# Dispatch of the last four bins: three quarters of the slots, instead of half, summed in the mixture and ahead of the third expert group

## The reference, cut to what matters

```python
x = x + gcn(layernorm(x))            # two GCN layers over 100000 edges, 6250 nodes, 768 features
xn = l2norm(layernorm(x))            # 6250 x 768
logits = xn @ phin                   # 6250 x 1024 (32 experts x 32 slots)
d_w = softmax(logits over slots of an expert)    # dispatch weights
c_w = softmax(logits over all 1024 slots)        # combine weights
slots = xn.T @ d_w                   # 768 x 1024, sum over all 6250 nodes   <- what is changed
h  = gelu(slots @ w1[e] + b1[e])     # per expert, hidden 384
eo = h @ w2[e] + b2[e]               # per expert, back to 768
x = x + c_w @ eo
```

## Time and profile before

| | us |
|---|---|
| median of 3 runs | 3303.42 (3299.69 to 3303.58) |
| the profiled execution, its own time | 3298.73 |
| its span | 3297.0 |
| PE busy | 3078.9 (93%) |
| DVE / ACT / POOL busy | 1898.3 / 1155.6 / 1869.7 |

### The profile page before, as it was taken

The page is one execution under the profiler, slowest core; times in us unless marked ns, Lnnn a source line. Parts: engine busy times, 40 slices in busy tenths (PEclk is TensorE's granted clock), DMA queues, the critical chain, the costliest instruction groups (busy, mean ns, idle before and its releaser), DMA issues. The chain is left out here.

```text
span 3297.0 us, 62639 instructions
## 1 busy us (share of the span) xinstructions
PE 3078.9 (93%) x21857; PEld 2070.2 (63%) x21857; DVE 1898.3 (58%) x3437; ACT 1155.6 (35%) x1578; POOL 1869.7 (57%) x1804
## 2 busy tenths in 40 slices
PE   3769999999999999789999999999999998689998
PEld 1347777878787878556666666666666653345665
DVE  7854545554444444277777777777777773102332
ACT  4842323233323232245444444444444441111000
POOL 3377777777777777377666666666666631100000
PEclk8989999999999999899999999999999999899999
DMA  8789999999999999599889998998999879998995
GB/s 310 271 320 372 335 340 332 340 337 331 339 335 340 339 341 331 184 336 348 309 308 311 308 310 309 309 310 307 309 309 311 309 250 338 315 327 230 268 229 141
DMA packets 344868, 1013.79 MB, mean 307 GB/s; under 512 B 147903, under 2 KB 157578, under 8 KB 335592
## 3 DMA queue, kind: packets, MB, share of 16 engines
q0 software_dynamic: 137376, 664.09, 57.5%
q1 hardware_dynamic: 195152, 312.01, 29.2%
q10 hardware_dynamic: 12040, 33.69, 3.2%
HBM read 873.96 MB, written 129.21 MB: 304 GB/s over the span
## 5 line engine op out<-in xcount | busy, mean ns | idle before, releaser
L1610 POOL DMA_INDIRECT xs<-table,idx x833 | 877.2, 1053 | 473.4 <-PE m_part L1787 277.1
L1065 POOL DMA_INDIRECT xs<-table,idx x833 | 899.1, 1079 | 306.8 <-issue 192.8
L1787 PE MATMUL m_part<-xs 128*128 128x512 f16 (+1 forms) x3332 | 585.6, 329 | 27.1 <-DMA xs<-table,idx 22.0
L1382 PE MATMUL a_part<-xs 128*128 128x512 f16 (+1 forms) x3332 | 591.3, 328 | 15.3 <-DMA xs<-table,idx 11.0
L1787 PEld LDWEIGHTS m_part<-xs 128*128 128x128 f16 x3332 | 417.8, 142 | 164.9 <-issue 43.3
L1382 PEld LDWEIGHTS a_part<-xs 128*128 128x128 f16 x3332 | 409.6, 142 | 135.2 <-issue 26.7
L1816 PE MATMUL m_ps_l<-xs,m_xT 128*128 128x512 f16 x1764 | 388.7, 379 | 0.4 <-issue 0.2
L1803 PE MATMUL m_ps_s<-dw_mem,xn_mem 128*128 128x512 f16 x1296 | 312.4, 381 | 3.1 <-DVE xs L1677 3.0
L1816 PEld LDWEIGHTS m_ps_l<-xs,m_xT 128*128 128x128 f16 x1764 | 172.0, 98 | 207.9 <-issue 1.5
L1332 PE MATMUL a_ps_o<-Ws,xs 128*128 128x512 f16 x1764 | 294.8, 326 | 1.3 <-ACT xs L1115 1.2
L1115 ACT ACTIVATE xs<-xs 128x128 f16<-128x128 f32 x294 | 88.6, 310 | 464.7 <-DVE xs L1266 460.4
(11 more groups left out here) (418 smaller groups left out, 3909.4 us busy)
## 6 DMA issues: line engine op xcount, KB each, us to landing
xs<-in_L_ffn_w_dram SPq DMA_DIRECT2D x64, 1152.0 KB, 10.3
xs<-table SPq DMA_DIRECT2D x98, 384.0 KB, 6.2
xs<-table,idx POOLq DMA_INDIRECT x1666, 5.8
cw_dram<-xs SPq DMA_DIRECT2D x49, 512.0 KB
table<-arena SPq DMA_DIRECT2D x49, 384.0 KB, 3.1
table<-xs SPq DMA_DIRECT2D x49, 384.0 KB, 4.7
xs<-x_pad SPq DMA_DIRECT2D x49, 384.0 KB, 6.1
x_dram<-xs SPq DMA_DIRECT2D x49, 384.0 KB, 5.5
```

The source lines that it names most:

```text
L1065: pool.indirect_dma_start(out=ring[:, t, :], out_offset=None, in_=table, in_offset=bass.IndirectOffsetOnAxis(ap=idx[:, k:k + 1], axis=0)). ...
L1382: mm = nc.tensor.matmul(part[:, bass.ds(to + a, z - a)], pick[:, i % 2, :, t], ring[:, n % RING, half * D + a:half * D + z], start=False, ...
L1610: pool.indirect_dma_start(out=ring[:, t, :], out_offset=None, in_=table, in_offset=bass.IndirectOffsetOnAxis(ap=idx[:, n:n + 1], axis=0)). ...
L1787: mm = nc.tensor.matmul(part[:, bass.ds(off + at, e - f)], pick[:, i % 2, :, t], ring[:, n % RING, half * D + f:half * D + e], start=False ...
```

## The change

The boundary between what `second_layer` sums for the last four bins and what the mixture sums moves from slot 512 to slot 256 (`LATE_AT`). In `second_layer` the 12 units of the last four bins get 256 columns instead of 512. In the mixture each late unit has 24 matmuls (512 and 256 columns in turn) instead of 12 of 512, and its add is 768 wide instead of 512. All six late units now stand behind `down_product(0)`, and `up_product(2)`, whose slots begin at 256, waits for all of them.

```diff
+LATE_AT = K // 4
...
+        def width(g):
+            return 512 if g < whole else LATE_AT
...
-                        v.tensor_tensor(slots[:, c, a:a + 512], slots[:, c, a:a + 512], ps_s[:, tile % 2, :], ALU.add).then_inc(added, 1)
+                        v.tensor_tensor(slots[:, c, a:a + width(g)], slots[:, c, a:a + width(g)], ps_s[:, tile % 2, 0:width(g)], ALU.add).then_inc(added, 1)
...
-                                mm = nc.tensor.matmul(ps_s[:, tile % 2, :], spread(xn[q % XN][:, xh, :], DC)[:, c, :], dw[:, q % DW, dh, a:a + 512],
+                                mm = nc.tensor.matmul(ps_s[:, tile % 2, 0:width(g)], spread(xn[q % XN][:, xh, :], DC)[:, c, :], dw[:, q % DW, dh, a:a + width(g)],
...
-        late_units = {0: (0, 1, 2), 1: (3, 4), 2: (5,)}
+        late_units = {0: range(DC)}
...
-                    v.tensor_tensor(slots[:, c, K // 2:K], slots[:, c, K // 2:K], ps_o[:, c % 2, 0:K // 2], ALU.add).then_inc(late_added, 1)
+                    v.tensor_tensor(slots[:, c, LATE_AT:K], slots[:, c, LATE_AT:K], ps_o[:, c % 2, 0:K - LATE_AT], ALU.add).then_inc(late_added, 1)
...
-                    if g == HG:
+                    if g == LATE_AT // P:
                         pe.wait_ge(late_added, DC)
...
-                            mm = nc.tensor.matmul(ps_o[:, c % 2, 0:K // 2], spread(xn[b % XN][:, xh, :], DC)[:, c, :], dw[:, b % DW, dh, K // 2:K],
-                                                  start=(b == LATE_BINS[0] and xh == 0 and dh == 0), stop=(b == LATE_BINS[-1] and xh == 1))
+                            for a, e in ((LATE_AT, LATE_AT + 512), (LATE_AT + 512, K)):
+                                mm = nc.tensor.matmul(ps_o[:, c % 2, a - LATE_AT:e - LATE_AT], spread(xn[b % XN][:, xh, :], DC)[:, c, :], dw[:, b % DW, dh, a:e],
+                                                      start=(b == LATE_BINS[0] and xh == 0 and dh == 0), stop=(b == LATE_BINS[-1] and xh == 1))
```

## The result

| | before | after |
|---|---|---|
| median of 20 runs, us | 3301.79 | 3306.69 |
| lowest, highest | 3293.87, 3308.03 | 3302.21, 3312.78 |
| profiled execution's time, span | 3298.73, 3297.0 | 3305.12, 3303.3 |

The ratio is 1.0016, 95% interval 1.001 to 1.0023: 4.9 us slower on the medians. The forecast was 1.6 us faster (3301.8), with a range up to 3306.5. Here "before" is the median of 20 runs; the forecast was added to the median of three, 3303.42.

A forecast was written before the change was run, and what follows sets the result against it. The prediction took the weight stream to bound the first four expert groups, and TensorE-VectorE handoffs the end of second_layer. -4.2 us there and +2.6 for an empty queue gave -1.6: 3303.42 to 3301.8 us, range 3298.0 to 3306.5.

The forecast's parts named there:

- Narrower units at the end: End of second_layer: shorter matmuls and adds make the last add end 4.2 us earlier.
- the bounds of 3.1 and 4.6: Gain at the block's end: 3.1 us if SyncE does not move, 4.6 if its moved last issue sets the end.
- First products: Start of the mixture: first up product keeps 5.77 us; nothing taken for earlier-issued biases, up to 1 us held against.
- rival B: Second_layer's gain smaller or lost in the first products (SyncE, clock, biases): 3304 to 3305.6 us; chance 0.23 together with D.
- Late units: Behind down product 0: six units of 3.90 us, 23.4 us in all; up product 2 waits about 1.2 us for VectorE.
- rival C: Added narrow matmuls in the late units cost up to 0.216 us each: 7.7 us more, 3309.5 us; chance 0.10.
- The load behind it: Down weights of group 2, requested after down product 1: queue runs dry at 2790.3, issue at 2791.2, 2.6 us lost.
- The sum: Whole kernel: -4.2 us from second_layer's end, +2.6 from the empty queue, together -1.6 us.
- the 0.2% to which the prediction gave 0.92: Whole kernel: chance 0.92 that the time stays within 0.2%, 6.6 us, of no change.

The follow-up runs named there:

- tail_only: Changed kernel with the mixture of before, so only second_layer's last four bins are summed 256 wide; ratio to before 0.9993 (0.9984 to 1.0002).
- order5: Changed kernel with turn 1 and down product 1 moved ahead of the sixth late unit and up product 2; ratio to before 1.0002 (0.9993 to 1.0011).
- fill: order5 with one late unit moved between up products 0 and 1; ratio to before 0.9993 (0.9984 to 1.0002).
- before_bias: Kernel before with the first expert group's hidden bias loaded at the end of second_layer; ratio to before 1.0004 (0.9995 to 1.0012).
- before_early: before_bias plus the third of second_layer's last four weight loads issued right behind the last write of cst; ratio to before 0.9997 (0.9988 to 1.0006).
- late_only: Changed kernel with second_layer of before (512 wide), so only the mixture's half of the change; ratio to before 1.0017 (1.0009 to 1.0026).
- after_early: Changed kernel with the first hidden bias and the third of second_layer's last four weight loads issued earlier; ratio to before 1.0001 (0.9992 to 1.001).

## Why the prediction was wrong, step by step

**Narrower units at the end.** Right: the adds end 4.0 us earlier (4.2 forecast; 3.5 to 3.6 in tail_only, order5 and fill). The block ends 3.5 us earlier, within the bounds of 3.1 and 4.6. In this trace that is because the landing of `cst` took 0.9 us longer and SyncE became the last; in the other three VectorE was the last and the gain was the same.

**First products: the step that failed.** "I take nothing for it and hold up to 1 us against it." Up product 1 waited 4.0 us instead of 0.67, and ran 1.7 us longer at the low clock. Down product 0 was forecast to end at 33.3 and ended at 39.0. The miss of 5.7 us is 0.7 (block end) + 3.3 (wait) + 1.7 (clock). I had followed SyncE's two last loads to their issue, as a thing that could end the block, but not to their landing, and had not asked who waits for it. up_product(1) does. In before they landed at 24.5, 3.7 us ahead of their user at 28.2 (some 2 us with up product 0 at the high clock). The gain of 3.5 us went nearly whole into this slack: the path to their issue leads through the softmax, the write of `cst` and its landing, and won 0.6 us here and 1.3 to 1.5 in tail_only, order5 and fill, and even there they landed no earlier than in before. The biases, issued 1.7 us behind SyncE's last issue instead of 4.7, share the engines with them: the later load needed 10.5 us instead of 7.6. The Trainium skill says that DMAs of the SP and POOL queues run on the same 16 engines and interleave (Trainium Kernel Development and Optimization, "Key Constraints"); the trace agrees (88.4% of the engines' time for the biases' queue, 25.8% for the weights', while the last weights were still out). The clock was named in rival B, but for the first up product; that it could fall at the second was not seen. The granted clock was 1.00 during the wait of 4.01 us and 0.50 from 2755 to 2757.

**Late units.** Right to 0.1 us: 144 matmuls in 23.54 us (23.4 forecast), so strided weights cost no time here, which ends rival C. Up product 2 waited 1.09 us (1.2 forecast). From the end of down product 0 to that of down product 1: 33.9 us forecast, 33.9 measured.

**The load behind it.** Right in kind, wrong in size. The request came at 72.9, not 67.2, and the hole was 6.5 us, not 2.5. The later request is inherited from the first products; that the queue did not run dry later with it is not. The prediction took the arrival of the up weights of group 3 (70.5 before) as the moment at which the queue would be empty without a new request. But in before the down weights of group 2 had been requested at 65.0 and shared the engines with them. Two kernels whose issues in the mixture agree within 0.02 us up to that request show it, before_bias and before_early; in the first it goes out 3.2 us earlier (2783.48 against 2786.67), and up product 3 gets its weights 1.6 us later:

```profile
2792.70 6.96 PE L2206 MATMUL e_ph<-xs 128*32 128x384 f32 x48 [9.27 <-DMA xs<-in_L_ffn_w_dram]
```

```profile
2791.07 6.24 PE L2207 MATMUL e_ph<-xs 128*32 128x384 f32 x48 [4.46 <-DMA xs<-in_L_ffn_w_dram]
```

So a late request loses more than the prediction's 2.6 us. In late_only, where nothing is inherited, the queue was empty from 66.5, down product 2 started 3.1 to 4.0 us late, and the time was 5.6 us longer (3.0 to 8.6).

**The sum.** Down product 2 was forecast at 84.3 and came at 90.6, 6.3 us late, and the time is 6.5 us over the forecast (4.9 + 1.6). after_early takes the first error away and keeps the second: down product 2 starts at 84.6, and the time is 0.3 us over before (-2.6 to +3.3) where -1.6 was forecast. So about 5 of the 6.5 us are the first products; the rest fits the term of the load, but is not clear of noise. The outcome is rival B's mechanism with a wait three times as long as I allowed, on top of the hole. The ratio, 0.16%, still lies within the 0.2% to which the prediction gave 0.92; that is the width of the bound and no merit of the sum.

The halves by themselves give 1.0017 x 0.9993 = 1.0010, the edge of the measured interval, and each has its own interval of about 0.09% to either side. That the two do a little more harm together (the low clock and the wait move the late units, and these the request) is likely and not shown.

## What to carry to other kernels

When the end of a stage comes earlier, list every transfer whose issue hangs on another chain than the one shortened, and follow it to its landing and to its first user: its slack there is the most that the shorter end can bring to that user. In a stage bound by loads, work on the engine is free up to the point where it delays the next request into a queue that still has something to do; so put the product that frees a single buffer ahead of the work that merely fills time (order5 gave back what the change had lost), and that work into waits that exist (fill; its gain over order5 is not clear of noise). And when a load arrives while a newer one is already under way, its arrival is later than the moment at which the queue would have been empty without the newer one.

## What was not expected of the hardware

The same two loads of 1152 KB, issued 0.6 us earlier, landed 2.3 us later (10.5 instead of 7.6 us for the later one), with eight bias loads issued 1.7 us behind them instead of 4.7. These biases are small in bytes and dear in time: 0.27 MB took 88.4% of the 16 engines' time over 1.3 us, while over 2743.5 to 2745.5 0.84 MB of weights took all of it over 2 us. And a wait of 4 us cost twice: the 48 matmuls behind it took 5.77 us instead of 4.08, with the granted clock at the lower of its two levels (1.2 of 2.4 GHz) in part of them; in fill, with 3.9 us of other matmuls in the same wait, they took 4.08.
